# Output projection of an attention kernel: 128-token tiles against four column tiles of 32 tokens, in halves over two steps

## The reference

```python
scores = jnp.einsum('bhsd,bhtd->bhst', q_embed, k_embed) / D ** 0.5
attn = jax.nn.softmax(scores, axis=-1)
out = jnp.einsum('bhst,bhtd->bhsd', attn, v)
out = out.transpose(0, 2, 1, 3).reshape(B_, S_, C)
return jnp.einsum('bsc,oc->bso', out, wo)
...
x = _layernorm(x + _L0_attn_ref(...), axis=-1)
...
_, topk_idx = jax.lax.top_k(gates, TOP_K)
pos = jnp.cumsum(expert_mask, axis=0) - 1
```

## Time and profile before

| | us |
|---|---|
| median of 3 runs | 943.03 |
| lowest and highest run | 940.41, 943.56 |
| profiled execution, first to last instruction | 943.4 |

### The profile page before, as it was taken

The page is one execution under the profiler, slowest core; times in us unless marked ns, Lnnn a source line. Parts: engine busy times, 40 slices in busy tenths (PEclk is TensorE's granted clock), DMA queues, the critical chain, the costliest instruction groups (busy, mean ns, idle before and its releaser), DMA issues. The chain is left out here.

```text
span 943.4 us, 19478 instructions
## 1 busy us (share of the span) xinstructions
PE 896.2 (95%) x7357; PEld 510.3 (54%) x7357; DVE 634.9 (67%) x1197; ACT 731.0 (77%) x894; POOL 478.1 (51%) x398
## 2 busy tenths in 40 slices
PE   9798899999999999999999999999589999999994
PEld 6333344444334443434443443334489999998993
DVE  5677456547787654788666577527547877888876
ACT  6588788877798889779789879998255787777873
POOL 0377243235657555647574454532523656666564
PEclk9999999989999999999999999999799999999998
DMA  6749742433347254343533524631273445534311
GB/s 178 240 165 325 257 155 75 151 102 114 118 175 260 74 180 157 127 160 134 191 110 116 188 97 167 198 94 53 81 240 119 136 147 180 168 124 143 132 61 56
DMA packets 63672, 140.25 MB, mean 149 GB/s; under 512 B 10306, under 2 KB 31363, under 8 KB 63440
## 3 DMA queue, kind: packets, MB, share of 16 engines
q1 hardware_dynamic: 42512, 74.98, 24.7%
q0 software_dynamic: 21056, 63.93, 19.2%
HBM read 71.95 MB, written 66.54 MB: 147 GB/s over the span
## 5 line engine op out<-in xcount | busy, mean ns | idle before, releaser
L760 ACT ACTIVATE prob<-spsum 128x1024 f32<-128x1024 f32 x512 | 493.4, 1022 | 101.7 <-PE spsum L966 97.4
L990 PE MATMUL opsum<-prob,val 128*17 128x512 f32 x2048 | 274.0, 605 | 3.9 <-DVE oraw L1365 2.2
L966 PE MATMUL spsum<-area_q 32*128 32x512 f32 x1536 | 133.6, 431 | 7.2 <-DMA area_q<-aT 3.6
L966 PEld LDWEIGHTS spsum<-area_q 32*128 32x128 f32 x1536 | 73.4, 187 | 121.9 <-ACT prob L760 66.0
L966 PEld LDWEIGHTS spsum<-stacks 32*128 32x128 f32 x1536 | 73.6, 183 | 112.9 <-ACT prob L760 62.6
L966 PE MATMUL spsum<-stacks 32*128 32x512 f32 x1536 | 132.9, 425 | 0.5 <-issue 0.5
L1373 DVE RECIPROCAL oden<-oden 128x256 f32<-128x256 f32 x62 | 108.7, 1753 | 2.1
L639 POOL TENSOR_TENSOR onorm<-oraw,oden 128x512 f32<-128x512 f32 x31 | 41.8, 1349 | 104.5 <-DVE oden L1373 101.6
L553 POOL TENSOR_TENSOR area_s<-emb,area_s 128x1024 fp32r<-128x1024 f32 x28 | 66.6, 2378 | 51.3 <-DVE area_s L1184 51.3
L597 POOL DMA_INDIRECT dispatched<-res,scatter_idx x64 | 65.0, 1015 | 48.5 <-PE spsum L966 24.5
L990 PEld LDWEIGHTS opsum<-prob,val 128*17 128x17 f32 x2048 | 36.3, 96 | 90.6 <-ACT prob L760 50.3
(11 more groups left out here) (244 smaller groups left out, 1359.4 us busy)
## 6 DMA issues: line engine op xcount, KB each, us to landing
split_scratch<-area_s POOLq DMA_DIRECT2D x60, 512.0 KB, 4.1
area_k<-in_w SPq DMA_DIRECT2D x16, 1024.0 KB, 5.3
stacks<-split_scratch SPq DMA_DIRECT2D x28, 512.0 KB, 5.4
area_q<-split_scratch SPq DMA_DIRECT2D x28, 512.0 KB
dispatched<-res POOLq DMA_DIRECT2D x1, 5300.0 KB, 26.0
rows<-dispatched SPq DMA_DIRECT2D x7, 662.5 KB, 4.6
res<-in_x SPq DMA_DIRECT2D x4, 1024.0 KB, 8.6
aT<-onorm SPq DMA_DIRECT2D x124, 32.0 KB
```

Of the source, the lines that this page charges most:

```text
L760: act.activation(prob[u % NPB][:], spsum[u % NSB][:].rearrange("p a n -> p (a n)"), ACT.Exp, scale=HD ** -0.5).then_inc(s_exp, 1)
L966: ins = pe.matmul(spsum[u % NSB][:, j % 2, :], kst[par][rows, a, P * kt:P * (kt + 1)], qst[par][rows, b, cols], start=i == 0, stop=i == 2 ...
L990: ins = pe.matmul(opsum[32 * j:32 * j + HD + 1, :], val[b % 2][:, kt, h0 + j, :], prob[(2 * s + j // 2) % NPB][:, HALF * (j % 2):HALF * (j ...
```

## The change

The product of a tile is written as four products per half of the contraction (k), each with 32 tokens as outputs in a column tile of its own. Where the new table `open` names an earlier step than `tile`, the first half (k = 0) runs in that step and the second in the step of `tile`; otherwise both run in one step. The steps of the three tails move: the last tile from 21 to 27 (26 in batch 2), `norm` from 24 to 29 (28), `top` from 28 to 33 (31), `place` from 34 to 37 (34 in batch 2), and `SPLIT_X` from 14 and 22 to 18 and 27. The four tiles of the last batch that lie in the loop keep their steps, in the new form.

```diff
@@ misc schedule and tables
+def opened_early():
+
+    at = {}
+    for u, (b, t0, _) in enumerate(UNITS):
+        t = TAIL[u]
+        for n, s in enumerate(t.get("open", ())):
+            if s < t["tile"][n]:
+                at[STEPS * GROUPS * (b + 1) + s] = ("tile", u, t0 + n)
+    return at
...
-LOOP = dict(tile=(10, 11, 12, 13, 15, 18, 19, 21), rstd=22, norm=24, exp=27, pairs=(25, 26, 29, 33), top=28,
-            place=34)
-TAIL = [LOOP] * (BATCH - 1) + [
+LOOP = dict(open=(10, 12, 15, 17, 19, 21, 24, 26), tile=(11, 13, 16, 18, 19, 21, 25, 27), rstd=28, norm=29, exp=31,
+            pairs=(29, 32, 33, 34), top=33, place=37)
+TAIL = [LOOP] * (BATCH - 2) + [
+    dict(open=(10, 12, 15, 17, 19, 21, 24, 26), tile=(11, 13, 16, 18, 19, 21, 25, 26), rstd=27, norm=28, exp=30,
+         pairs=(28, 29, 30, 31), top=31, place=34),
...
-        SPLIT_X = (14, 22)
+        SPLIT_X = (18, 27)
...
+            def tile_part(job, k):
+
+                _, u, i = job
+                b = UNITS[u][0]
+                if k == 0:
+                    begin(job)
+                    pe.wait_ge(s_aT, 16 * GH * (2 * GROUPS * (b + 1) if b < BATCH - 1 else 2 * NG - 2))
+                for j in range(GH):
+                    tok = P * i + 32 * j
+                    ins = pe.matmul(bank(job)[32 * j:32 * (j + 1), 0:TOKEN], aTs[b % 2][:, k, tok:tok + 32],
+                                    woT[:, k, :], start=k == 0, stop=k == KC - 1)
+                return ins
+
             def run(job):
                 kind, c, i = (*job, 0)[:3]
                 misc = bank(job)
-                begin(job)
+                if kind != "tile":
+                    begin(job)
...
-                    b = UNITS[c][0]
-                    pe.wait_ge(s_aT, 16 * GH * (2 * GROUPS * (b + 1) if b < BATCH - 1 else 2 * NG - 2))
-                    for k in range(KC):
-                        ins = pe.matmul(misc[:, 0:TOKEN], aTs[b % 2][:, k, P * i:P * (i + 1)], woT[:, k, :],
-                                        start=k == 0, stop=k == KC - 1)
+                    for k in range(1 if job in opened.values() else 0, KC):
+                        ins = tile_part(job, k)
...
                     scores(s, shifted)
+                    if s in opened:
+                        tile_part(opened[s], 0)
                     for job in jobs_at(s):
                         run(job)
```

More of the change, by code:

```diff
@@ L106, in build @@
     jobs = misc_schedule()
+    opened = opened_early()
     soft_at = softplus_steps(jobs)
@@ L127, in build @@
         areas = (area_k, area_q, area_s)
-        attention(nc, jobs, soft_at, number, first, last, x_d, xT_d, wq_d, wk_d, wv_d, wo_d, bias_d, wr_d,
+        attention(nc, jobs, opened, soft_at, number, first, last, x_d, xT_d, wq_d, wk_d, wv_d, wo_d, bias_d, wr_d,
                   br_d, trig_d, ident_d, tri_d, blocks_d, rev_d, base_d, blank_d, number_d, wop_d, woz_d, w1_d,
@@ L141, in weight_views, with attention @@
     return raw1, raw2, w1s, w2s
-def attention(nc, jobs, soft_at, number, first, last, x_d, xT_d, wq_d, wk_d, wv_d, wo_d, bias_d, wr_d, br_d,
+def attention(nc, jobs, opened, soft_at, number, first, last, x_d, xT_d, wq_d, wk_d, wv_d, wo_d, bias_d, wr_d, br_d,
               trig_d, ident_d, tri_d, blocks_d, rev_d, base_d, blank_d, number_d, wop_d, woz_d, w1_d, w2_d,
```

## The result

| | before | after |
|---|---|---|
| median of 4 runs each, us | 943.3 | 961.8 |
| lowest and highest run | 940.4, 945.5 | 960.7, 963.2 |
| profiled execution, first to last instruction | 943.4 | 958.9 |

The ratio is 1.0184 (95% interval 1.0160 to 1.0207): the change makes the kernel 18.5 us slower by the medians, 15.5 by the two profiled executions. The forecast was 954.3 with a range of 941 to 960. The sign was right, the size was 7.5 us short by the medians.

The account below looks back on a forecast made before the run. ScalarE was taken to bound plain steps, TensorE tile steps, with VectorE late in the tails. Terms -5.1 - 3.9 + 6.0 + 0.3 + 0.9 + 13.1 = +11.3 us gave 954.3, range 941 to 960.

Parts of the forecast that it names:

- the sum of the tail, +13.1: Steps 33 to 38: new waits for VectorE's output copy and placement read, 2 x (2.3 + 3.0) + 2.5 us.
- The product, -5.1: Output tiles as column products, a half at 0.48 us: 5.1 us given back if nothing waits.
- Step 17, +6.0: Opening tile 3 waits 2.0 us in each of three tails for VectorE to read tile 2.
- -1.5 for step 19: Step 19: the wait for the read of the tile before goes, 1.5 us over the three tails.
- the rival's price: Rival that VectorE keeps pace everywhere: step 17 also finds its bank free, 6.0 us less, 935.2; chance 0.06.
- T16: Start of step 16; tile 2's bank forecast free at T16 + 5.24, wanted by TensorE at T16 + 3.28.
- Step 21, +0.3: Step 21: the wait for the norms' read stays, 0.1 us longer in each tail.
- softplus, +0.9: Step 11: ScalarE's extra 1.06 us is not fully covered by a half step, 0.3 us per batch.
- The waits that go at 25 and 33, -2.4: Tails 0 and 1: TensorE's waits for the copy of attention outputs in steps 25 and 33 vanish, 2.4 us.
- The chains: VectorE's queue reckoned operation by operation from tile 7 to the copy of step 32 and the placement's read.
- T27: Start of step 27 in batches 0 and 1, zero of their chain: variances end at 5.5, copy 17.5, placement's bank free 30.7.
- its rival: Rival that GpSimd doesn't hold the variances: step 33's wait of 2.3 goes in tails 0 and 1, 949.7; chance 0.20.

Follow-up runs that it names:

- form: The kernel before with each output tile as four column products of 32 tokens, all in its one step, nothing moved; ratio 0.9987 to the kernel before.
- no17: The changed kernel with tile 3 made whole in step 18 instead of opened in step 17; ratio 1.0201 to the kernel before.
- whole: The changed kernel with no tile opened early, all eight tiles of a batch made whole in the steps where they end; ratio 1.0179 to the kernel before.
- order16: The changed kernel with VectorE reading tile 2 in step 16 ahead of its branch on the flag; ratio 1.0154 to the kernel before.
- warm: The changed kernel with TensorE's waits in the three steps 33 and step 38 of the first tail filled by 8 unread products; ratio 1.0167 to the kernel before.
- nolow: The changed kernel with GpSimd's product of the second split cut to one column in the first two tails; ratio 1.0104 to the kernel before.

## Why the prediction was right and wrong

The step that failed is the sum of the tail, +13.1. From step 33 on, the tails moved by 18.5 us where that term, less the waits that go, gave 11.9. It priced every wait by its length alone, which puts TensorE's clock behind the wait at nothing without a reason: 3.3 us. And it had VectorE's queue behind the copy of step 32 too short: 2.9 us. The terms one by one:

- **The product, -5.1.** The half was priced at 0.48 and took 0.47; half steps last 2.34 for 2.37. By the rule of the Trainium skill that was weighed ("TensorE: Matmul & The Clock Gate", Part 3: Packing small matmuls) it would have been 0.57; the page's figure is for row tiles of 512 columns, and for column tiles of 264 the trace doesn't agree. Wrong was that its gain was booked in full beside VectorE's waits: `form` shows most of it taken back in steps 15, 19 and 25 of the first two tails. In the changed kernel this didn't show in the sum, since there the waits of 19 and 25 had been given terms of their own.
- **Step 17, +6.0, "the surest term", and -1.5 for step 19.** Length, place and cause of the wait were right: 4.25 to 4.27 in the three tails. As a loss of its own it was wrong. `no17`, `whole` and `order16` take it or most of it away, and steps 10 to 19 gain nothing. What failed here is the rival's price, which the sum doesn't use: with the bank free at T16 + 3.3 the time was to be 6.0 lower, and by these steps it is the same, because the prediction followed VectorE's queue to the read of tile 2 and not on to that of tile 3.
- **Step 21, +0.3, and softplus, +0.9.** Step 21 lasts 3.49 for 3.46. Step 13 lasts 2.73, 0.38 over a half step, for 0.3.
- **The waits that go at 25 and 33, -2.4.** Step 25 of tails 0 and 1 lasts 2.35, a plain half step, as forecast. In step 33 one wait went and a longer one came, which the next term has.
- **The tail, +13.1.** The chains were good up to the copy: the variances end 5.5 after T27 (5.5 forecast), the copy at 17.8 (17.5), in tail 2 at 18.8 (18.6); the waits in 33 are 2.5, 2.5 and 2.8 for 2.3, 2.3 and 2.5. Behind the copy the queue was later than reckoned: two pairs took 4.6 for 3.7, and the placement's bank is free at 32.4 for 30.7. That alone would have made the mask's wait in step 37 2.2 for 0.5, as `warm` shows. The variance beside GpSimd was the right side of its rival, shown by `nolow`.
- **What failed most: no term for TensorE's clock.** Each wait was priced by its length. In the profiled execution four of the five waits of 2.3 us and more in steps 33 and 38 were followed by 3.4 us at half clock. At full price in two: 1.5 in step 38 of tail 0 and 1.4 in steps 33 and 34 of tail 2, both by the runs that filled these waits and by `whole`, which had them without a fall. In part or not at all in the other two: in tail 1 the start of step 38 came 0.4 earlier in `warm`, in tail 0 not at all, since the mask was later still. So the 6.5 us from step 33 on are, as far as single executions tell: 3.3 clock; 1.7 and 1.2 by which the placement's bank came free later than reckoned; 0.3 the longer wait of tail 2.
- **Not seen: step 30.** ScalarE's `rstd`, now in 28, waits for the blocked variances, and step 30 lasts 4.12 for 3.48 in two tails; `nolow` gives 0.37 of that back. Other small terms, such as half steps of 2.34 for 2.37, balance it, so it is in part luck that steps 10 to 32 come out as forecast.
- **Not seen: the first batch.** `SPLIT_X` moves there too, where no tail needs it. In step 22 TensorE waits 3.5 for GpSimd's L599 and is at half clock behind it, 8.30 for 3.48 us. It costs nothing: the waits for transfers in steps 31 and 32, and their half clock, shrink, and both kernels start step 35 92.9 us after step 1. So right by luck.
- **The medians.** They moved 3 us more than the profiled executions. Two things can make that, and no run parts them. The four runs of before may be a low draw, since the same kernel had 946.2 to 946.9 elsewhere. Or the profiled pair flatters the change: of the four runs of the changed kernel the profiled one is the fastest and has the highest mean clock (0.979, the others 0.973 and 0.974), and the profiled one of before had 6.8 us at half clock in steps 2 to 4, where most of the others that fell had 3.4.

## What to carry to other kernels

Follow a late queue to its end: a wait that you add or take away in the middle of it is no loss or gain before the next thing that wants the queue is looked at, and its price is the difference at the point where the queue is empty again. Here a wait of 2.0 us taken out in the middle changed nothing. Price a stall of TensorE of 1.5 us or more by its length and a chance of slow products behind it, and look in the profile's clock row for the stalls that the kernel has already. Where another engine is late at a fixed place, put the work that it must read ahead of that place: eight numbers in a table were worth more here than the new form of the product.

## What the runs showed of the hardware

- Behind some waits of TensorE the granted clock went to 0.5 for 3.4 us, at a price of 1.4 to 1.5 us where TensorE was the bound. Waits of 1.46 (`warm`, step 17), 1.71, 2.06 and 2.48 us were followed by it, others of 2.49 and 2.97 were not, and the same step did it in one execution and not in another. The Trainium skill ("TensorE: Matmul & The Clock Gate", section Why this matters for your kernels) advises against idle gaps of more than about 3 us between bursts; here shorter ones already did it.
- The clock also fell with no wait ahead of it: in steps 2 to 4 of tail 0, while TensorE was busy all the time with products of 8 columns, in the kernel before and in several variants, and not in this execution of the changed kernel.
- A VectorE operation of 8 columns stood for 2.27 us beside a GpSimd product of 2.45 that began 0.2 earlier, and took 0.17 without it.
- Four fp32 column products of 32 outputs and 264 columns take 0.47 us, and a whole tile in this form stands 0.91 between scores and values, against 1.09 for the product of 128 outputs.
